# One order for every attention step, outputs four steps behind their turn, and a shorter lead of the row maxima

## The reference

```python
x = L0_attn_q                                  # (8, 512, 256) float32
x = x + 0.5 * ffn(layernorm(x))                # down(silu(gate) * up), hidden size 768, int32 weights / 127
x = x + attn(layernorm(x))
x = x + 0.5 * ffn(layernorm(x))

def attn(q):                                   # 16 heads of 16
    qh, kh, vh = heads(q @ Wq.T), heads(q @ Wk.T), heads(q @ Wv.T)
    scores = qh @ kh.T / 4 - slope[head] * abs(i - j)
    out = softmax(scores) @ vh
    return out @ Wo.T + bo
```

## Time and profile before

| what | value |
|---|---|
| median of 3 runs | 933.65 us (932.74 to 934.33) |
| the profiled execution | 935.75 us, span 934.0 us, mean granted clock 0.942 |
| busy share of the span | PE 91%, PEld 54%, DVE 70%, ACT 56%, POOL 46% |
| chain that ended last | PE 66%, DVE 22%, issue 4%, ACT 4%, POOL 2% |
| DVE, reduction of one maxima tile | 684 ns each, 512 of them |
| DVE, one division of heads | 244 ns and 716 ns |
| DVE, split of `xt`; negation | 693 ns; 354 ns and 362 ns |
| ACT, stage copy; cast | 590 ns; about 620 ns |
| POOL, fix; split | 735 ns; about 1280 ns |

### The profile page before, as it was taken

One profiled execution on the slowest core, in us unless ns is written; L12 is line 12 of the kernel. 1 busy time (PEld: TensorE's weight loads), 2 busy tenths in 40 slices (PEclk: granted clock), 3 DMA queues, 4 the chain that ended last, 5 costly groups with the idle time before them and its releaser, 6 DMA issues.

```text
span 934.0 us, 13035 instructions
## 1 busy us (share of the span) xinstructions
PE 846.5 (91%) x4576; PEld 505.9 (54%) x4576; DVE 657.8 (70%) x1359; ACT 520.5 (56%) x745; POOL 426.7 (46%) x486
## 2 busy tenths in 40 slices
PE   2999999769999899899899899899899897999998
PEld 2778887624344344444444444443444335888886
DVE  5898888376776776777676777776767645677774
ACT  4444444305577676577576577676567585344442
POOL 0445344323445644554654654653644464434443
PEclk9999999956799999899899999998889899999999
DMA  9320000562450450550540540540504000001001
GB/s 358 101 24 2 3 2 3 68 89 30 55 70 19 52 69 13 59 67 8 65 64 7 69 61 11 69 61 10 69 18 52 2 2 2 25 25 48 25 25 46
DMA packets 21490, 43.17 MB, mean 46 GB/s; under 512 B 3848, under 2 KB 5912, under 8 KB 21208
## 3 DMA queue, kind: packets, MB, share of 16 engines
q1 hardware_dynamic: 21400, 41.92, 26.2%
HBM read 12.02 MB, written 4.62 MB: 18 GB/s over the span
## 4 chain that ended last, share of the span: by engine, by line
PE 66%; DVE 22%; issue 4%; ACT 4%; POOL 2%; DMA 1%; SPq 1%; DVEq 0%; ACTq 0%
PE ps L977 61%; DVE row_max L895 9%; DVE hid L791 3%; PE ps L989 1%; PE ps L1033 1%; DVE xn L753 1%; ACT stage L648 1%; DVE newton L730 1%; PE ps L1014 1%; POOL att_t L522 1%; PE ps L1038 1%; DMA k_aug<-parts 1%; DVE mean_var L712 1%; SPq L442 1%; DVE var L722 1%
## 5 line engine op out<-in xcount | busy, mean ns | idle before, releaser
L895 DVE TENSOR_REDUCE row_max<-ps 128x1 f32<-128x512 f32 x512 | 328.8, 684 | 153.0 <-PE ps L977 153.0
L686 ACT ACTIVATE probs<-ps 128x1024 f32<-128x1024 f32 x256 | 254.8, 1023 | 79.6 <-PE ps L977 78.3
L567 POOL TENSOR_TENSOR probs<-probs,diag 128x256 f32<-128x256 f32 x256 | 187.6, 735 | 214.9 <-ACT probs L686 214.7
L977 PE MATMUL ps<-k_aug,q_aug 60*128 60x512 f32 x512 | 183.1, 514 | 32.3 <-DVE row_max L895 17.9
L502 POOL TENSOR_TENSOR hid_r<-hid,hid_r 128x512 fp32r<-128x512 f32 x96 | 125.0, 1304 | 176.4 <-ACT hid_r L594 165.4
L977 PE MATMUL ps<-xnt,wgu_r 128*128 128x512 f32 x768 | 189.6, 401 | 12.9 <-DVE hid L791 8.1
L977 PEld LDWEIGHTS ps<-xnt,wgu_r 128*128 128x128 f32 x768 | 143.0, 190 | 53.2 <-DVE hid L791 15.1
L977 PEld LDWEIGHTS ps<-k_aug,q_aug 60*128 60x128 f32 x512 | 77.5, 200 | 160.3 <-DVE row_max L895 131.1
L977 PE MATMUL ps<-probs,v_aug 128*32 128x512 f32 x1024 | 149.3, 658 | 1.8 <-POOL probs L567 1.8
L600 ACT ACTIVATE gated<-ps 128x512 f32<-128x512 f32 x96 | 57.4, 598 | 119.4 <-PE ps L977 119.4
L977 PE MATMUL ps<-q_aug,k_aug 62*128 62x512 f32 x512 | 122.7, 467 | 1.0 <-ACT probs L686 1.0
(11 more groups left out here) (63 smaller groups left out, 681.4 us busy)
## 6 DMA issues: line engine op xcount, KB each, us to landing
q_aug<-parts SPq DMA_DIRECT2D x96, 128.0 KB, 4.6
k_aug<-parts SPq DMA_DIRECT2D x96, 128.0 KB, 6.4
x_sb<-x_in SPq DMA_DIRECT2D x8, 512.0 KB, 12.4
x_out<-x_sb SPq DMA_DIRECT2D x8, 512.0 KB, 2.6
diag<-diag_table SPq DMA_DIRECT2D x1, 2048.0 KB, 19.1
wgu_i<-w_gate_up SPq DMA_DIRECT2D x2, 768.0 KB, 6.6
w_att<-w_att SPq DMA_DIRECT2D x1, 1024.0 KB, 11.6
q_aug<-max_row SPq DMA_DIRECT2D x64, 8.0 KB
```

What stands on the lines that cost most here:

```text
L567: nc.gpsimd.tensor_tensor(tile, tile, diag[:, kt % 2, n * QH + 2 * pair:n * QH + 2 * pair + 2, :], ALU.mult).then_inc(fixed, 1)
L686: nc.scalar.activation(probs[:, kt % 2, 2 * pair:2 * pair + 2, :], ps[:, at:at + 2, :], ACT.Exp, scale=SLOPE_UNITS[pair]).then_inc(exp_don ...
L895: nc.vector.reduce_max(row_max[:, quad % 2, u % 2, u // STEPS, (u % STEPS) // 2:(u % STEPS) // 2 + 1], max_bank(b, tile)[0], mybir.AxisLis ...
L977: return nc.tensor.matmul(out, lhs, rhs, start=start, stop=stop, **k)
```

## The change

- FILLS: every even step has one fill, no odd step has one except the max fills at s = 5. `turn1_prev` moves from (0,7) to (1,2), `out0_prev` from (1,1) to (1,6), `out1_prev` from (1,6) to (2,0), `turn0` from (2,7) to (3,6); `qk1_next` moves from (0,6) to (1,0), `qk3_next` from (2,6) to (3,0), `v0_next` from (3,1) to (2,2), `v1_next` from (3,4) to (3,2).
- `pieces` and `spread_tiles` go. Each step is: score pair, two maxima tiles, then the values (odd steps), then the whole fill where there is one.
- MAX_LEAD goes from 28 to 26.
- Before the first turn DVE runs `apply_kept` ahead of all maxima, and no longer behind the first four tiles.

```diff
--- before.py
+++ after.py
@@ -115,10 +115,10 @@
 
 
 FILLS = {
-    (0, 0): "xt0_next", (0, 1): "xt1_next", (0, 3): "heads3_prev", (0, 4): "max1", (0, 5): "qk0_next",
-    (0, 6): "qk1_next", (0, 7): "turn1_prev", (1, 1): "out0_prev", (1, 3): "heads0", (1, 5): "max2",
-    (1, 6): "out1_prev", (2, 3): "heads1", (2, 4): "max3", (2, 5): "qk2_next", (2, 6): "qk3_next",
-    (2, 7): "turn0", (3, 1): "v0_next", (3, 3): "heads2", (3, 4): "v1_next", (3, 5): "max0_next",
+    (0, 0): "xt0_next", (0, 2): "xt1_next", (0, 4): "heads3_prev", (0, 5): "max1", (0, 6): "qk0_next",
+    (1, 0): "qk1_next", (1, 2): "turn1_prev", (1, 4): "heads0", (1, 5): "max2", (1, 6): "out0_prev",
+    (2, 0): "out1_prev", (2, 2): "v0_next", (2, 4): "heads1", (2, 5): "max3", (2, 6): "qk2_next",
+    (3, 0): "qk3_next", (3, 2): "v1_next", (3, 4): "heads2", (3, 5): "max0_next", (3, 6): "turn0",
 }
 ALL_FILLS = list(FILLS.values())
 
@@ -134,44 +134,8 @@
 
 
 
-WEIGHT_SCORES, WEIGHT_VALUES = 0.6, 1.0
-WEIGHTS = {"heads": 0.6, "max": 0.2, "turn": 0.55, "xt": 0.55, "qk": 1.4, "v": 1.7, "out": 1.7}
 MAX_TILES = 2 * NQ * STEPS
-MAX_LEAD = 28
-
-
-def pieces(n, s):
-
-
-    if s % 2 == 0:
-        return ("scores", "half0", "half1")
-    if (n, s - 1) in FILLS:
-        return ("scores", "values", "half0", "half1")
-    return ("scores", "half0", "half1", "values")
-
-
-def spread_tiles():
...
-TILES_AT = spread_tiles()
+MAX_LEAD = 26
 
 
 
@@ -941,23 +905,20 @@
                 else:
                     ln_apply(at, 0, range(TT))
 
-            row_maxima(0, -MAX_LEAD, 4 - MAX_LEAD)
             apply_kept(1, range(TT))
-            row_maxima(0, 4 - MAX_LEAD, 0)
+            row_maxima(0, -MAX_LEAD, 0)
 
             def turn(b):
                 made = 0
                 for n in range(NQ):
                     for s in range(STEPS):
-                        count = sum(TILES_AT[n, s])
                         if n == 1 and 2 <= s < 6:
                             if b + 2 < B:
                                 apply_kept(b + 2, (s - 2,))
                             elif b + 2 == B:
                                 first_rows(s - 2)
-                        row_maxima(b, made, made + count // 2)
-                        row_maxima(b, made + count // 2, made + count)
-                        made += count
+                        row_maxima(b, made, made + 2)
+                        made += 2
                         name = FILLS.get((n, s))
                         if name in fills_of(b) and name.startswith(HEADS):
                             divide(b, name)
@@ -1176,15 +1137,14 @@
                                          q_aug[b % 2][rows, 2 * n + pair, :], True, True)
                         ins.then_inc(st_done, 1)
                         name = FILLS.get((n, s))
-                        for piece, count in zip(pieces(n, s), TILES_AT[n, s]):
-                            if piece == "values" and s > 1:
-                                weigh_values(quad_no, n, (s - 3) // 2, b)
-                            elif piece == "values" and not (first(b) and n == 0):
-                                weigh_values(quad_no - 1, (n - 1) % NQ, TT - 1, b)
-                            elif piece.startswith("half") and name in fills_of(b):
-                                fill(b, name, (int(piece[-1]),))
-                            scores_for_max(b, made, made + count)
-                            made += count
+                        scores_for_max(b, made, made + 2)
+                        made += 2
+                        if s > 1 and s % 2 == 1:
+                            weigh_values(quad_no, n, (s - 3) // 2, b)
+                        elif s == 1 and not (first(b) and n == 0):
+                            weigh_values(quad_no - 1, (n - 1) % NQ, TT - 1, b)
+                        if name in fills_of(b):
+                            fill(b, name)
 
             for b in range(B):
                 turn(b)
```

More of the change, by code:

```diff
@@ L132 @@
 TAIL_AT = {0: "heads3_prev", 2: "turn1_prev", 4: "out0_prev", 5: "out1_prev"}
-WEIGHT_SCORES, WEIGHT_VALUES = 0.6, 1.0
-WEIGHTS = {"heads": 0.6, "max": 0.2, "turn": 0.55, "xt": 0.55, "qk": 1.4, "v": 1.7, "out": 1.7}
 MAX_TILES = 2 * NQ * STEPS
-MAX_LEAD = 28
-def pieces(n, s):
-    if s % 2 == 0:
-        return ("scores", "half0", "half1")
-    if (n, s - 1) in FILLS:
-        return ("scores", "values", "half0", "half1")
-    return ("scores", "half0", "half1", "values")
-def spread_tiles():
-    def weight(n, s, piece):
-        if piece.startswith("half"):
-            return WEIGHTS[FILLS[n, s].split("_")[0][:-1]] / 2 if (n, s) in FILLS else 0
-        return WEIGHT_SCORES if piece == "scores" else WEIGHT_VALUES
-    steps = [(n, s) for n in range(NQ) for s in range(STEPS)]
-    whole = sum(weight(n, s, piece) for n, s in steps for piece in pieces(n, s))
-    done, made, out = 0.0, 0, {}
-    for n, s in steps:
-        out[n, s] = []
-        for piece in pieces(n, s):
-            done += weight(n, s, piece)
-            until = 2 * int(MAX_TILES // 2 * done / whole + 1e-6)
-            out[n, s].append(until - made)
-            made = until
-    assert made == MAX_TILES
-    return out
-TILES_AT = spread_tiles()
+MAX_LEAD = 26
 SPLIT_POOL, SPLIT_DVE, HEADS, OUT = ("qk", "turn"), ("xt",), ("heads",), ("out",)
```

## The result

After the change the kernel takes 895.66 us (median of 4 runs, 892.01 to 898.40), against 933.19 (928.71 to 934.33, 4 runs) before: a ratio of 0.9604, interval 0.9557 to 0.9651. The profiled execution took 898.40 us, its span is 896.6 us and its mean granted clock 0.966 (before 0.942).

The account below looks back on a forecast made before the run. It took PE to bound the kernel, with 56.1 us of work per turn plus waits, mostly in maxima pairs for DVE. -18 - 4 - 3.5 - 1 + 2 = -24.5 gave 910 us, range 897 to 927.

Parts of the forecast that it names:

- Order in a step: Six full turns, two maxima tiles right behind each score pair: 3.0 us less per turn, -18 us, bounds -9 and -24.
- The walk: Step-by-step sum of PE's waits through one turn: 9.2 us of waits, turn 65.3 us at full clock against 68.4.
- The 1.69 before out0: PE's wait before out0 for POOL's split of the turn, 1.69 us, forecast to go in seven turns.
- Lead: Before the first turn, normalisations ahead of all maxima (-2.4) and two tiles fewer (-1.6): together -4 us.
- Row maxima: Scores at (0,0) may wait for max0_next's DMA behind qk3's rows: 0 to 1.5 us per turn, taken as 0.3, +2.
- Rival D: Row maxima's DMAs land late, behind the last rows: +1.5 x 7 = +10 us, about 918; chance 0.07.
- First turn: First attention turn, which has no previous outputs: 0 to -2 us; first and last turn together taken as -3.5.
- Clock: Attention part's lost clock: -6.7 for spells behind out0, +5.4 for short steps, net -1 us, between -15 and +15.
- +5.4: Low-clock spells in the short steps, (3,4) to (0,5), cost about 5.4 us; the stretch doubles, so +5.4 us.
- rival C: The clock comes back, with nearly no spells left: 15 to 19 us more gained, about 895; chance 0.17.
- rival A: Clock stays low in the short steps, (3,4) to (0,5): slower, 945, about 975 at worst; chance 0.08.
- rival B: Waits only change place: -18 becomes -3, about 925, or 931 with late row maxima; chance 0.08.

Follow-up runs that it names:

- e1_lead: The kernel before with only MAX_LEAD 26 and the four normalisations ahead of all maxima: 936.8 us, ratio 1.0084.
- e6_rows: The changed kernel with qk2 at (2,2), qk3 at (2,6), v0 at (3,0), and qk2's rows issued ahead of max3: 910.64 us, ratio 0.9777.
- e7_both: The changed kernel with the edits of e6_rows and POOL's add_bo moved from (1,0) to (2,3): 905.01 us, ratio 0.9717.
- e2_table: The kernel before with only the new table of fills, tiles still spread by weight and fills still cut: 914.06 us, ratio 0.9844.
- e3_even: The changed kernel with the old table of fills, keeping the even order and lead 26: 993.39 us, ratio 1.0679.
- e8_out: The kernel before with only out0 moved to (1,6) and out1 to (2,0): 934.12 us, ratio 1.0030.

## Why the prediction was right and wrong

- **Direction and path: right.** The sum was made on starts of PE, DVE and POOL, and every wait that it named at a new place is there. It gave no value for one of 0.69, at (1,4).
- **Order in a step: right, a little over-priced.** The walk gave 65.3 us per turn at full clock; the turns at 1.00 take 65.44 to 66.70, and 65.3 to 66.1 where the values' wait for POOL at (1,3) is gone too. The 1.69 before out0 is gone. Single waits, forecast against the third turn by starts: (0,1) 0.6 and 0.61, (0,2) 0.9 and 0.91, (0,4) 1.4 and 1.4, (1,3) 1.4 and 1.15, (1,5) 0.65 and 0.69; (1,6) was over-priced, 0.75 and 0.27. The order is worth about 14.0 us in six turns, forecast 16.3.
- **Lead: right in size, wrong as an independent term.** The -4 came (-5.0, of which e1_lead shows 4.0 alone). "cost 0.3 to 1.3 there, once" was wrong: the lead also decides in which step the negation falls, in every turn. In the old order lead 26 costs 16.5 us of waits at max fills in eight turns, in the new one lead 28 costs about 1.4 us in each of the first five full turns (67.8 on the mean against 66.5).
- **Row maxima: right in kind, under-priced.** 4.6 us of waits in eight places, forecast 2 (0.3 per turn, with bounds 0 and 1.5); single ones are 0.3 to 1.25. The Trainium skill (DMA: Bandwidth & Descriptors, "Queues, rings and completion order") has descriptors of one ring consumed in order. The runs agree in kind: at most 2.83 us from issue to scores on an empty queue, 3.86 where the last rows were issued 3.4 us earlier, 4.75 right behind them. Rival D's full price, 1.5 per turn, was only reached in e6_rows and e7_both.
- **First turn: under-forecast.** -3.7 for "0 to -2": its clock rose from 0.84 to 0.89.
- **Clock: the step that failed.** The prediction set -6.7 for the spells behind out0 against +5.4, because the stretch of short steps "becomes twice as long", and got -1; 13.4 us came. The first half was about right: the 8.5 lost us right behind out0 are gone. The step that failed is the +5.4: instead of doubling, the 6.8 lost us in the stretch of short steps (5.4 us of time) went to nothing, so that this term had the wrong sign. It took the sum of waits over the whole stretch for what draws a spell. In the changed kernel the stretch holds about as much waiting as the walk said (4.3 us in the third turn, 4.8 forecast), hardly more than before (4.2 in the second turn), and none of six full turns has a spell there; with the same table and the old spreading (e2_table) five of six have one, where a wait of 1.15 stands right beside one of 0.70. The walk had a wait for each step, and could have been read for waits that stand close together. What exactly counts in such a passage stays open, since the even order both parts the waits and shortens them. The spells that were left in the first five full turns came from the one such place that the prediction had named and priced only as a wait, (1,3). The other 10.2 lost us of before stood at (1,5) and behind it in three turns, and the prediction's sum had no term for them; 8.6 are left in that part of the turns.
- **The spell at 504 to 508** The earlier trace rows was the prediction's reason against rival C: it stood "without a long pause". It did, and by starts that turn had waits of 0.4, 0.3, 0.6, 0.3 and 0.6 close together between 498.4 and 504.4, so the likely cause is the one seen in e2_table; but the same waits had a spell behind them in only three of six full turns, and no run took these waits alone away. Rival C had the outcome and the time of 895, but its reason is only half of it: e2_table has no long pause either, and kept its spells.
- **Rivals A and B** did not happen, but parts of the change do just what they say: the even order on the old table (e3_even) is rival A, first by DVE's waits and then by the clock, and the outputs alone (e8_out) are rival B, waits that only change place.
